# A two-layer graph network on one core: the per-group sums, one-hots and window finishing are placed ahead of VectorE's wait for the gathered rows, and half of the attribute products behind the V products

## The chip, the core and the metric

The kernel runs on one core of a Trainium2 chip. A core has TensorE (PE in the profile; PEld is its weight loading), VectorE (DVE), ScalarE (ACT), GpSimd (POOL) and the sync engine SP, which here only issues DMAs. Each engine runs its own program in order and waits on semaphores. The metric is the device time of one execution in microseconds. Before the change it is 3113.4 us, the median of three runs (3105.56 to 3114.23).

## What is computed

A graph of 6250 nodes with 128 features and 200,000 edges sorted by destination. Layer 0 is a graph attention layer with 4 heads; layer 1 sums edge attributes and neighbours and runs a two-layer perceptron. Cut to what matters:

```python
h = relu(layernorm(x))                              # layer 0
xp = (h @ W).reshape(n, 4, 32)                      # the rows called V
e = leaky_relu(a_s[src] + a_d[dst], 0.2)            # self loops are added to the edges
e = exp(e - segment_max(e, dst)[dst])
out = segment_sum(e * xp[src], dst) / segment_sum(e, dst)
x = x + relu(out + bias)
h = relu(layernorm(x))                              # layer 1
edge_agg = segment_sum(edge_attr @ We + be, dst)
x_comb = concatenate([h, edge_agg])
z = x_comb + segment_sum(x_comb[src], dst)
x = x + relu(z @ W1 + b1) @ W2 + b2
```

## The kernel before the change

The program first makes the table of rows xp with their logits, then runs over the edges in 87 groups, and at the end multiplies a stored adjacency matrix with the layer-1 rows (49 windows, the last stage). The change lies in the loop over groups; everything else stays.

A group is 2304 edges, laid out as 128 partitions by J = 18 columns. Since the edges are sorted, the destinations of a group fall in a window of 128 nodes, and neighbouring groups' windows overlap, so the running sums of a window are loaded from DRAM, changed and stored again by each group. Buffers of V, AT (attributes), SEL (the one-hot matrix) and node alternate between two (b is n mod 2); `state`, the 128 x 261 tile of a window's running sums, exists once. Its columns are 128 weighted feature sums, 4 sums of weights and a count (133, `TAB`), and 128 attribute sums (to `ST` = 261).

For group n the work goes like this:

- POOL gathers the rows of V with 18 indirect DMAs. Its last ones (j = 14, 15, 16) wait until the V products of group n - 1 have passed each of their three quarters (`vm_b`).
- DVE waits for the gather, copies the logits (`logit`) and runs a segmented maximum over them: a scan, a carry across partitions by way of PE (`tailT`, `tails`, `cback`), and a second scan. The peaks are split into three bf16 parts, and PE reduces them into the window's nodes (`mg`, 18 matmuls with the one-hot `selH`).
- DVE makes the new shifts (`newold`, `nu`, `node`) and splits them. PE looks them up for each edge (`look`, 18 matmuls with `selT`). DVE and ACT turn them into weights (`lks`, `lin`, `lre`, `wps`), and DVE multiplies V by them in three quarters (`vw_b`).
- PE sums by one-hot matmuls: the attribute products (`attribute_sums`, L1133: SEL times AT, 18 columns in fp32, two passes each in the trace) and the V products (L1194: SEL times V). Between them stand chunks of the adjacency matrix (`adjacency`, L1123 and L1125), each evacuated by ACT.
- When group n + 1 is under way, DVE finishes group n: `rescale_state` multiplies the loaded state by the fold factors, `add_sums` adds the products (`merged`), and a chain of small dependent steps (`finish_weights` to `finish_shift`, with three Newton rounds for a reciprocal square root) makes the next layer's rows.

In the kernel before, DVE does all of this behind the logit copy of group n + 1, woven between the steps of the maximum: `select` and `rescale_state` stand behind the first scan, `add_sums` behind the `tails` scan, and the finishing steps one by one between the later ones.

SP's program sets when transfers start. In an item it issues in this order: store of the state of n - 1 (waits for `merged`), store of the new peaks, indices for n + 2, peaks and rows for n + 1 (waits for `look`), **the attributes for n + 2** (L453, 1152 KB, waits for `am_b` of group n, the end of the attribute products), **the state of group n** (L502, 130.5 KB), x of the window (L505), and then the stores of the finished rows and of the adjacency block. The order is that of the code:

```python
if ahead is not None:
    load_attributes(n + 2, b, ahead)    # after(sp, s("am_b"), n, 2)
...
load_sums(n, base)                      # state <- sums0
```

`rescale_state(n)` in turn begins with two waits:

```python
dve.wait_ge(s("s_load"), n * 16 + 16)   # the state of group n has landed
after(dve, s("fold_b"), n)
```

## Time and profile before

| | |
|---|---|
| median of 3 runs | 3113.4 us (3105.56 to 3114.23) |
| the profiled execution | 3102.13 us, span 3100.2 us |
| PE busy, DVE busy | 66%, 58% of the span |
| ACT busy, POOL busy | 35%, 54% |
| mean granted TensorE clock | 0.764 of full speed |
| moved by DMA | 560.29 MB, mean 181 GB/s |
| group loop | 87 groups, about 2.5 ms of the span |
| last stage | from about 2660 us to the end |

Busy time is time in which an engine has an instruction running. Where an engine is neither full nor empty, what counts is which wait ends last in each group. A timeline row shows start, duration, engine, line and tiles, and in brackets the idle time before it with what ended it. Rows of matmuls are merged with their count (x30 is 15 columns of two passes).

### The profile page before, as it was taken

What the parts mean: (1) busy time and instruction counts of PE and PEld (TensorE: products, weight loads), DVE (VectorE), ACT (ScalarE), POOL (GpSimd) and SP (SyncE); (2) the same over time, 40 slices, a digit from 0 to 9 for tenths busy, and PEclk for the clock granted to TensorE, in tenths of its full rate; (3) what the DMA queues carried; (4) which work ended last, traced back from release to release, by engine and by line L of the source; (5) the groups of instructions that cost most, each with busy time, mean ns of one, the idle gap of its engine ahead of it and who ended that gap; (6) DMA issues with size and microseconds to landing.
All of it is one profiled execution on the core that took longest, in us unless ns stands there. A gap on an engine that the chain in (4) does not pass through costs nothing.

```text
span 3100.2 us, 64216 instructions
## 1 busy us (share of the span) xinstructions
PE 2043.0 (66%) x16208; PEld 1674.9 (54%) x16208; DVE 1807.2 (58%) x6198; ACT 1085.6 (35%) x2295; POOL 1673.2 (54%) x1626
## 2 busy tenths in 40 slices
PE   4365665665665655665656656656656656699998
PEld 3354554554554544554545545545545544588887
DVE  7566676665666666666666766766766766411111
ACT  3134344344434443443443443443444443300000
POOL 4566666666666666666666666666666666000000
PEclk8677777776777767777767777777777777799999
DMA  9855655655655555655556556556556555666654
GB/s 192 134 163 177 194 168 174 195 159 180 193 155 187 177 169 189 189 160 185 162 176 194 157 184 194 168 173 194 156 185 194 156 185 176 225 213 214 225 212 146
DMA packets 276907, 560.29 MB, mean 181 GB/s; under 512 B 113395, under 2 KB 211139, under 8 KB 248081
## 3 DMA queue, kind: packets, MB, share of 16 engines
q1 hardware_dynamic: 226763, 444.37, 42.5%
q0 software_dynamic: 50112, 115.56, 16.5%
q8 instruction: 12, 0.20, 0.0%
q14 instruction: 20, 0.16, 0.0%
HBM read 382.53 MB, written 177.22 MB: 181 GB/s over the span
## 4 chain that ended last, share of the span: by engine, by line
PE 41%; issue 20%; DVE 15%; DMA 9%; another core or an unknown queue 5%; SPq 3%; ACT 2%; POOL 2%; ACTq 1%; DVEq 1%; POOLq 0%
PE pv L1133 10%; PE pv L1248 9%; DMA big<-table,idx 8%; PE pv L1194 7%; PE pt L1248 4%; PE pt L1123 3%; PE pm L1161 2%; POOL big L816 2%; ACT xsb L852 2%; PE pa L1123 1%; DVE peaks L1513 1%; DVE tabb L1477 1%; PE pa L1177 1%; ACTq L905 1%
## 5 line engine op out<-in xcount | busy, mean ns | idle before, releaser
L816 POOL DMA_INDIRECT big<-table,idx x1566 | 1639.8, 1047 | 929.9 <-issue 414.2
L852 ACT ACTIVATE xsb<-pt 128x343 f32 x1042 | 477.8, 459 | 1213.3 <-PE pt L1125 567.1
L1133 PE MATMUL pv<-big 128*128 128x128 f32 x3132 | 523.6, 336 | 5.7 <-ACT big L852 3.5
L1133 PEld LDWEIGHTS pv<-big 128*128 128x128 f32 x3132 | 490.3, 246 | 36.1 <-issue 11.7
L1123 PE MATMUL pt<-tabb 128*128 128x343 bf16 x1042 | 400.0, 384 | 65.8 <-ACT xsb L852 36.5
L1194 PE MATMUL pv<-big 128*128 128x133 f32 x3132 | 391.3, 280 | 7.0 <-DVE big L1742 4.2
L1638 DVE COPY logit<-big 128x72 f32<-128x72 f32 x87 | 21.9, 252 | 608.6 <-DMA big<-table,idx 540.1
L1194 PEld LDWEIGHTS pv<-big 128*128 128x128 f32 x3132 | 367.8, 190 | 16.2 <-DVE big L1742 8.6
L1477 DVE TENSOR_TENSOR tabb<-iotah,keyp 128x2064 bf16<-128x2064 bf16 x261 | 319.7, 1225 | 0.0
L1142 PE MATMUL pm<-ident,pre 128*4 128x128 f32 x87 | 32.5, 374 | 433.9 <-DVE pre L1643 226.5
L1248 PE MATMUL pv<-big,xsb 128*128 128x384 bf16 (+1 forms) x1617 | 279.3, 330 | 18.5 <-DVE big L1779 18.5
L852 ACT ACTIVATE xsb<-pa 128x343 f32 x521 | 238.9, 458 | 95.0 <-ACT xsb L852 50.3
L1248 PEld LDWEIGHTS pv<-big,xsb 128*128 128x128 bf16 (+1 forms) x1617 | 230.4, 147 | 52.4 <-issue 21.4
L1142 PEld LDWEIGHTS pm<-ident,pre 128*4 128x4 f32 x87 | 7.2, 82 | 451.5 <-DVE pre L1643 236.4
L1742 DVE TENSOR_TENSOR big<-big,pm 128x768 f32<-128x768 f32 x261 | 233.4, 949 | 26.2 <-ACT pm L852 18.7
L1125 PE MATMUL pt<-tabb 128*128 128x49 bf16 x1041 | 224.9, 216 | 0.0
L1123 PE MATMUL pa<-tabb 128*128 128x343 bf16 x521 | 200.8, 385 | 28.3 <-issue 18.3
L1161 PE MATMUL pm<-peaks,selb 128*128 128x13 bf16 x1566 | 56.2, 174 | 228.8 <-DVE peaks L1513 143.7
L1123 PEld LDWEIGHTS pt<-tabb 128*128 128x128 bf16 x1042 | 114.9, 110 | 159.5 <-ACT xsb L852 63.1
L1161 PEld LDWEIGHTS pm<-peaks,selb 128*128 128x128 bf16 x1566 | 48.5, 105 | 261.2 <-DVE peaks L1513 157.2
L852 ACT ACTIVATE big<-selb 128x2304 f32<-128x2304 bf16 x87 | 184.1, 2116 | 1.0 <-DVE selb L1477 1.0
L852 ACT ACTIVATE fhT<-pt,b1s 128x128 f32<-128x128 f32 (+1 forms) x49 | 18.0, 367 | 388.6 <-PE pt L1225 388.6
(289 smaller groups left out, 2975.8 us busy)
## 6 DMA issues: line engine op xcount, KB each, us to landing
adj<-xsb SPq DMA_DIRECT2D x87, 1568.0 KB
big<-in_edge_attr_dram SPq DMA_DIRECT2D x87, 1152.0 KB
xsb<-adj SPq DMA_DIRECT2D x33, 1568.0 KB, 6.2
selb<-rel SPq DMA_DIRECT2D x87, 576.0 KB
tabb<-adj SPq DMA_DIRECT2D x16, 1568.0 KB, 6.2
big<-table,idx POOLq DMA_INDIRECT x1566
state<-sums SPq DMA_DIRECT2D x87, 130.5 KB
sums<-state SPq DMA_DIRECT2D x87, 130.5 KB
```

Source lines behind the costliest of these rows:

```text
L816: pool.indirect_dma_start(out=V[b][:, j, 0:rows], out_offset=None, in_=table, in_offset=bass.IndirectOffsetOnAxis(ap=index[b][:, j:j + 1], ...
L852: return nc.scalar.activation(out_, in_, func, **kw).then_inc(s(name), 1)
L905: _, at = nc.values_load_multi_w_load_instructions(offs[0:1, bass.DynSlice(n * OW + lo, hi - lo)], engines=[mybir.EngineType.Activation], ...
L1123: ins = nc.tensor.matmul(pab[c % 3], ohl[:, c, :], ohk[:, c, 0:KW], start=True, stop=alone)
L1125: ins = nc.tensor.matmul(pab[c % 3][:, 0:NB], ohl[:, (c - 1) % J, :], ohc[:, (c - 1) % J, 0:NB], start=False, stop=True)
L1133: ins = nc.tensor.matmul(sumA[b], SEL[b][:, j, :], AT[b][:, j, :], start=(j == 0), stop=(j == J - 1))
L1142: nc.tensor.transpose(tailT, pre1[:, :, J - 1], ident[:, :]).then_inc(s("tailT_b"), 1)
L1161: ins = nc.tensor.matmul(mg, selH[:, j, :], peaks[:, j, :], start=(j == 0), stop=(j == J - 1))
L1194: ins = nc.tensor.matmul(sumV[b], SEL[b][:, j, :], V[b][:, j, 0:TAB], start=(j == 0), stop=(j == J - 1))
L1248: ins = nc.tensor.matmul(pay[k][0:rows, 0:NK * C], adjT[k][:, 0:rows, h], yb[:, h, :], start=(h == 0), stop=(h == NB - 1))
L1477: return v.tensor_tensor(to.rearrange("p j (w e) -> p j w e", e=2), v_in, at, ALU.is_equal)
L1742: v.tensor_tensor(v4, v4, wps[:, js, :].rearrange("p j (h a) -> p j h a", a=1) .to_broadcast([128, QUART, H, F]), ALU.mult).then_inc(s("vw ...
```

## The change

Three things change in the code of a group.

1. The attribute sums get a PSUM bank of their own (`pc`), a single one in place of two halves of the alternating V banks. So the first attribute product of group n waits until group n - 1 is merged (before: n - 2), and the merge is two additions, one of 133 columns from `pv` and one of 128 columns from `pc`; the second waits for `am_b`.
2. Of the 18 attribute columns, 9 to 17 go behind the V products; `am_b` is signalled there.
3. On DVE `select`, the copy of the last-of-segment marks, `rescale_state`, `add_sums`, `finish_projection` and all finishing steps go ahead of the wait for the gathered rows.

```diff
@@ -286,7 +286,7 @@
         sumV = [pv[b][:, 0:TAB] for b in range(2)]
-        sumA = [pv[b][:, TAB:ST] for b in range(2)]
+        sumA = pc[:, 0:C]
@@ -1130,7 +1130,7 @@
                     for j in range(lo, hi):
-                        ins = nc.tensor.matmul(sumA[b], SEL[b][:, j, :], AT[b][:, j, :],
+                        ins = nc.tensor.matmul(sumA, SEL[b][:, j, :], AT[b][:, j, :],
                                                start=(j == 0), stop=(j == J - 1))
@@ -1165,7 +1165,7 @@
-                after(pe, s("merged"), n, 2)
+                after(pe, s("merged"), n, 1)
                 attribute_sums(0, 3)
@@ -1179,7 +1179,7 @@
-                attribute_sums(3, J).then_inc(s("am_b"), 1)
+                attribute_sums(3, 9)
                 if finish_before:
                     transpose_window(n - 1)
@@ -1194,6 +1194,7 @@
                     ins.then_inc(s("vm_b"), 1)
+                attribute_sums(9, J).then_inc(s("am_b"), 1)
                 if not is_extra:
                     adjacency(n, 9, 15)
@@ -1532,8 +1533,11 @@
             def add_sums(n, b):
                 dve.wait_ge(s("vm_b"), n * QN + QN)
-                dve.wait_ge(s("ms_b"), n * 2 + 2)
-                v.tensor_tensor(state[:, :], state[:, :], pv[b][:, 0:ST], ALU.add).then_inc(s("merged"), 1)
+                dve.wait_ge(s("ms_b"), n * 3 + 2)
+                v.tensor_tensor(state[:, 0:TAB], state[:, 0:TAB], pv[b][:, 0:TAB], ALU.add).then_inc(s("ms_b"), 1)
+                after(dve, s("am_b"), n)
+                dve.wait_ge(s("ms_b"), n * 3 + 3)
+                v.tensor_tensor(state[:, TAB:ST], state[:, TAB:ST], sumA, ALU.add).then_inc(s("merged"), 1)
@@ -1634,6 +1638,22 @@
+                select(n, b, extra_group)
+                last = isl[:, bass.DynSlice(g, 1), :].rearrange("p a (j c) -> p (a j) c", c=1)
+                v.tensor_copy(peaks[:, :, NK * H:NK * H + 1], last).then_inc(s("pkl_b"), 1)
+                if m is not None:
+                    rescale_state(m, 1 - b)
+                    add_sums(m, 1 - b)
+                if not (is_extra or (isinstance(n, int) and n < 2)):
+                    finish_projection(n - 2)
+                for step in (finish_weights, finish_mean, finish_bias, finish_residual, finish_stats,
+                             finish_variance, finish_eps, finish_halve, finish_guess, finish_b2):
+                    between(step)
+                for r in range(3):
+                    between(newton_square, r)
+                    between(newton_factor, r)
+                    between(newton_step, r)
+                between(finish_shift)
                 dve.wait_ge(s(f"gat{b}"), it * 16 * J + 16 * J)
                 v.tensor_copy(logit[:, :, :], V[b][:, :, C:C + H].rearrange("p j h -> p h j"))\
                     .then_inc(s("log_b"), 1)
@@ -1643,81 +1663,52 @@
-                select(n, b, extra_group)
-                if m is not None:
-                    rescale_state(m, 1 - b)
                 after(dve, s("thru_c"), n)
                 after(dve, s("tailT_b"), n)
                 v.tensor_tensor_scan(tails[:, 1:129], thruT[:, :], tailT, -BIG, ALU.add, ALU.max)\
                     .then_inc(s("tails_b"), 1)
-                if m is not None:
-                    add_sums(m, 1 - b)
-                if not (is_extra or (isinstance(n, int) and n < 2)):
-                    finish_projection(n - 2)
-                between(finish_weights)
-                between(finish_mean)
...
-                between(newton_step, 2)
-                between(finish_shift)
```

On DVE, the order around the wait for the gathered rows of the second group (the semaphores waited for stand in brackets; `gat1` is the gather, `s_load` the landing of the state). Before:

```order
L1635 TENSOR_SCALAR cont<-isl 128x4x17
L1638 COPY logit<-big 128x72 [waits gat1]
L1643 SCALAR_TENSOR_TENSOR pre<-cont,logit 128x72 [waits log_b,cont_b]
L1477 TENSOR_TENSOR selb<-iotah,drp 128x2304 [waits selc_b,mg_b]
L1528 TENSOR_TENSOR state<-state,fold 128x128 [waits fold_b,s_load]
L1530 TENSOR_TENSOR state<-state,fold 128x4
L1651 SCALAR_TENSOR_TENSOR tails<-thruT,pm 4x128 [waits tailT_b,thru_c]
L1536 TENSOR_TENSOR state<-state,pv 128x261 [waits ms_b,vm_b]
L1545 RECIPROCAL frd<-state 128x4 [waits merged]
```

The same place now, up to the first finishing steps; the logit copy comes only behind all of them:

```order
L1639 TENSOR_SCALAR cont<-isl 128x4x17
L1478 TENSOR_TENSOR selb<-iotah,drp 128x2304 [waits selc_b,mg_b]
L1643 CAST peaks<-isl 128x18
L1529 TENSOR_TENSOR state<-state,fold 128x128 [waits fold_b,s_load]
L1531 TENSOR_TENSOR state<-state,fold 128x4
L1537 TENSOR_TENSOR state<-state,pv 128x133 [waits ms_b,vm_b]
L1540 TENSOR_TENSOR state<-state,pc 128x128 [waits ms_b,am_b]
L1549 RECIPROCAL frd<-state 128x4 [waits merged]
L1551 COPY fdeg<-state 128x1
L1555 TENSOR_TENSOR fo<-state,frd 128x128 [waits fin]
```

The waits for `s_load` and `am_b` now stand in front of the wait for the gather, on the same engine.

On PE, the place behind the last quarter of V products in a group of the first pair (`pc` is the new bank, L1133 the attribute products, L1123 and L1125 the next adjacency chunk):

```order
 L1114 MATMUL pa<-wew,fhT 128x128
 L1194 MATMUL pv<-big 128x133 x6
+L1133 MATMUL pc<-big 128x128 x9
 L1123 MATMUL pt<-tabb 128x343
 L1125 MATMUL pt<-tabb 128x49
```

Nine columns of attribute products have come between the V products and the adjacency chunks.

SP's order is the same in both programs. The part of it on which the state load depends:

```order
L491 DMA selb<-rel 128x2304 [waits look]
L453 DMA big<-in_edge_attr_dram 128x2304 [waits am_b]
L502 ISA [waits ftr_f,s_store]
L502 DMA state<-sums 128x261
L505 ISA [waits x1_f]
L505 DMA fxw<-in_x_dram 128x128
```

Nothing moved here, but `am_b` is now signalled later.

## Rows read from the trace of the kernel before

**Rows 1.** Of the page: busy time and share of each engine
```profile
PE 2043.0 (66%) x16208; PEld 1674.9 (54%) x16208; DVE 1807.2 (58%) x6198; ACT 1085.6 (35%) x2295; POOL 1673.2 (54%) x1626
```

**Rows 2.** Of the page, costliest groups: columns are busy us, mean ns, idle before
```profile
L1638 DVE COPY logit<-big 128x72 f32<-128x72 f32 x87 | 21.9, 252 | 608.6 <-DMA big<-table,idx 540.1
```

**Rows 3.** Instructions on the tile state (ns min/median/max, first to last start)
```profile
L1528 DVE TENSOR_TENSOR state<-state,fold x87: 277/284/293, 152.1 to 2650.4; 128x128 f32<-128x128 f32 x87
...
DMA to landing us min/median/max: 1.7/5.4/12.2
```

**Rows 4.** Timeline of DVE, one group (start us, duration us, [idle before])
```profile
1528.42 0.22 DVE L1638 COPY logit<-big 128x72 f32<-128x72 f32 x1 [8.10 <-DMA big<-table,idx]
...
1528.98 1.34 DVE L1477 TENSOR_TENSOR selb<-iotah,drp 128x2304 bf16<-128x2304 bf16 x1
...
1530.51 0.40 DVE L1651 TENSOR_TENSOR_SCAN tails<-thruT,pm 4x128 f32<-4x128 f32 x1
...
1541.43 0.61 DVE L1725 TENSOR_REDUCE lks<-pa 128x144 f32<-128x432 f32 x1 [0.88 <-remote]
...
1543.44 2.68 DVE L1742 TENSOR_TENSOR big<-big,pm 128x768 f32<-128x768 f32 x3 [0.30 <-ACT pm L852]
...
1557.36 0.22 DVE L1638 COPY logit<-big 128x72 f32<-128x72 f32 x1 [7.39 <-DMA big<-table,idx]
```

**Rows 5.** Timeline of PE, the same group
```profile
1529.12 0.38 PE L1142 MATMUL pm<-ident,pre 128*4 128x128 f32 x1 [5.24 <-DVE pre L1643]
...
1530.97 0.59 PE L1144 MATMUL pm<-ident,tails 4*128 4x4 f32 x2 [1.48 <-issue]
...
1536.18 1.62 PE L1133 MATMUL pv<-big 128*128 128x128 f32 x6 [0.24 <-ACT big L852]
...
1538.29 0.66 PE L1177 MATMUL pa<-node,selb 128*128 128x24 bf16 x18 [0.49 <-DVE node L1511]
...
1539.76 4.87 PE L1133 MATMUL pv<-big 128*128 128x128 f32 x30
...
1545.20 2.97 PE L1194 MATMUL pv<-big 128*128 128x133 f32 x24
...
1548.45 1.53 PE L1194 MATMUL pv<-big 128*128 128x133 f32 x12
```

**Rows 6.** Timeline of ACT, the same group
```profile
1533.82 2.12 ACT L852 ACTIVATE big<-selb 128x2304 f32<-128x2304 bf16 x1
```

**Rows 7.** Timeline of SP's queue, the same group
```profile
1546.53 0.33 SPq L453 DMA_DIRECT2D big<-in_edge_attr_dram  x1
1547.21 0.33 SPq L502 DMA_DIRECT2D state<-sums  x1
```

**Rows 8.** Of the page, DMA issues: KB each, last number median us to landing
```profile
xsb<-adj SPq DMA_DIRECT2D x33, 1568.0 KB, 6.2
```

**Rows 9.** Timeline of SP's queue in the last stage
```profile
2740.93 0.34 SPq L593 DMA_DIRECT2D xsb<-adj  x1
2741.91 0.33 SPq L597 DMA_DIRECT2D state<-sums  x1
```

**Rows 10.** Windows of the last stage: engines, clock, DMA share, GB/s
```profile
2744.00:2745.00 1.00, 1.00 (x8) 0.87 (x7) 0.00 (x0) 0.00 (x0) 0.00 (x0) 1.00 0.94 401
```

**Rows 11.** Timeline of SP's queue, group 86 (no attribute load ahead of it)
```profile
2648.26 0.35 SPq L502 DMA_DIRECT2D state<-sums  x1
```

**Rows 12.** Timeline of DVE behind the last group
```profile
2650.40 0.29 DVE L1528 TENSOR_TENSOR state<-state,fold 128x128 f32<-128x128 f32 x1
...
2653.21 0.43 DVE L1536 TENSOR_TENSOR state<-state,pv 128x261 f32<-128x261 f32 x1 [2.44 <-PE pv L1194]
...
2658.28 0.16 DVE L1609 SCALAR_TENSOR_TENSOR fnm<-fmv,fy 128x1 f32<-128x1 f32 x1
```

**Rows 13.** Windows of the group: third number from the end is PEclk
```profile
1525.00:1526.00 1.00, 0.00 (x0) 0.00 (x0) 0.00 (x0) 0.27 (x1) 0.70 (x2) 0.69 0.97 376
...
1542.00:1543.00 1.00, 1.00 (x9) 1.00 (x8) 0.86 (x5) 0.66 (x3) 0.82 (x1) 0.78 0.46 92
```

More of the change, by code:

```diff
@@ L1661, in item @@
                                        in1=logit[:, :, 0], op0=ALU.add, op1=ALU.max).then_inc(s("carry_b"), 1)
-                between(finish_bias)
                 after(dve, s("carry_b"), n)
@@ L1666, in item @@
                     .then_inc(s("pre2_b"), 1)
-                between(finish_residual)
-                last = isl[:, bass.DynSlice(g, 1), :].rearrange("p a (j c) -> p (a j) c", c=1)
-                v.tensor_copy(peaks[:, :, NK * H:NK * H + 1], last).then_inc(s("pkl_b"), 1)
                 after(dve, s("pre2_b"), n)
@@ L1672, in item @@
                                 last.to_broadcast([128, J, H]), ALU.mult).then_inc(s("pk_b"), 1)
-                between(finish_stats)
                 split_peaks(n, 0)
-                between(finish_variance)
                 split_peaks(n, 1)
-                between(finish_eps)
                 split_peaks(n, 2)
-                between(finish_halve)
                 split_peaks(n, 3)
-                between(finish_guess)
                 if not is_extra:
@@ L1684, in item @@
                     v.tensor_scalar(selT, selT, ranko[:, 0:1], None, ALU.is_equal).then_inc(s("selt_b"), 1)
-                between(finish_b2)
-                between(newton_square, 0)
                 after(dve, s("mg_b"), n)
@@ L1692, in item @@
                                 AX.X, ALU.add).then_inc(s("mgs_b"), 1)
-                between(newton_factor, 0)
                 dve.wait_ge(s("st_load"), n * 32 + 32)
@@ L1698, in item @@
                     .then_inc(s("mnew_b"), 1)
-                between(newton_step, 0)
                 after(dve, s("mnew_b"), n)
@@ L1704, in item @@
                                 ALU.add).then_inc(s("nu_b"), 1)
-                between(newton_square, 1)
                 after(dve, s("nu_b"), n)
@@ L1708, in item @@
                                        op0=ALU.mult, op1=ALU.max).then_inc(s("sh_b"), 1)
-                between(newton_factor, 1)
                 split_shift(n, b, 0)
-                between(newton_step, 1)
                 split_shift(n, b, 1)
-                between(newton_square, 2)
                 split_shift(n, b, 2)
-                between(newton_factor, 2)
                 split_shift(n, b, 3)
```

## Prediction

> **What bounds the kernel now.** I read the busy shares first: no engine is full, PE has 66% and DVE 58% [rows 1]. So a group's time is a chain of waits, and I looked for the waits that end last. DVE sits idle before the logit copy for 608.6 us in 87 groups, 7.0 us each, nearly all of it released by the gather [rows 2]. The state tile's first rescale runs once a group, from 152.1 to 2650.4 us: 86 intervals of 29.05 us [rows 3]. Then I took one group of the timelines apart, from logit copy (T) to logit copy, 28.94 us:
>
> - T = 1528.42 to the lookup matmuls (L1177) at 1538.29: 9.87 us [rows 4, 5].
> - Lookups to the first V product (L1194) at 1545.20: 6.91 us [rows 5].
> - First V product to the next logit copy at 1557.36: 12.16 us, in which DVE waits 7.39 us for the gather [rows 4, 5].
>
> The state load is nowhere in this chain. It is issued at 1547.21 [rows 7], and the state is first needed behind the 1.34 us one-hot that follows the next logit copy [rows 4].
>
> **The change, part by part.**
>
> *Finishing ahead of the gather.* Behind T less work stands between the steps of the maximum. PE's transpose of the scan (L1142) ends at 1529.12 + 0.38 = 1529.50, but the tails scan starts only at 1530.51, behind the 1.34 us one-hot and the rescale [rows 4, 5]. Without them it starts at about 1529.52: 0.99 us won. From there ACT and PE bind. The carry matmul (L1144) starts at 1530.97; ACT's copy of the one-hot ends at 1533.82 + 2.12 = 1535.94; the first attribute products start at 1536.18 and take 1.62 us, so the lookups can't start before 1537.80, that is 0.49 us ahead of today's 1538.29 [rows 5, 6]. The rest of the moved work, some 5 us of DVE time, gains nothing more, since that copy ends last. Together 9.87 - 0.99 - 0.49 = 8.4 us from T to the lookups.
>
> *Half of the attribute products behind the V products.* DVE is ready with the first quarter of V 1541.43 - 1538.29 = 3.14 us (lookup read) + 2.01 us (to 1543.44) + a third of 2.68 us = 6.0 us behind the lookups [rows 4, 5]; with its signal 6.1 us. Today PE comes at 6.91 us, because 30 attribute passes of 4.87 us stand before [rows 5]. With 12 passes there DVE binds: 6.1 us, 0.8 won. The V products take 1548.45 - 1545.20 + 1.53 = 4.78 us, unchanged. Behind them now come 18 passes of 2.97/24 = 0.124 us (the spacing of the 24 V passes, which run at the full clock [rows 5]): 2.2 us. So `am_b` comes 7.0 us behind the first V product; today it comes at 1539.76 + 4.87 = 1544.63, which is 0.6 us ahead of it. It is 7.6 us later against the V products, 6.8 us against the lookups.
>
> *What hangs on am_b.* SP waits for it before the attribute load and issues the state load only behind that. DVE now waits for the state, and for `am_b` itself, ahead of the logit copy. Queued behind that wait on DVE are the merge, all finishing steps, the logit copy and the whole softmax chain, and PE, ACT and SP wait for these. From am_b on:
>
> - am_b to the issue of the attribute load: 1546.53 - 1544.63 = 1.9 us here [rows 5, 7]. SP had other work before in some groups, so I take 1.2 us, from both sides 0.5 and 2.0.
> - Attribute load to landing. A 1568 KB load lands a median of 6.2 us behind its issue [rows 8]; at the 401 GB/s of a full microsecond [rows 10] the 416 KB less take 1.0 us off: 5.2 us for 1152 KB.
> - The state load follows 0.68 us behind on the same queue [rows 7]. Alone it takes at most 2.1 us: issued at 2648.26 with no attribute load ahead, used at 2650.40 [rows 11, 12]. Loads of state behind a large load land in a median of 5.4 us, 1.7 to 12.2 [rows 3]; one is issued 0.98 us behind such a load [rows 9], so it lands 6.4 us behind it, right after the large load's own 6.2. I take 5.2 + 0.3 = 5.5 us behind the attribute load's issue. The ends for the range are 0.68 + 2.1 = 2.8 us and, by the long landings, about 8.5 us.
> - 0.2 us until DVE starts, an estimate.
> - DVE from the rescale to the logit copy. Behind the last group the same steps stand alone: from the addition at 2653.21 to the last step at 2658.28 is 5.07 us [rows 12]. Before them come the rescale (0.4 us to the first addition) and a second addition (0.3 us). Together 5.8 us.
>
> First V product to logit copy: 7.0 + 1.2 + 5.5 + 0.2 + 5.8 = 19.7 us, against 12.16 today. The gather is ready at 12.16 as before and is hidden.
>
> The Trainium skill (DMA: Bandwidth & Descriptors, Queues, rings and completion order) says that each DMA engine takes the descriptors of one ring in order; the trace agrees, with 6.4 us for the small load against 6.2 for the large one. Its table of measured transfers (same page, Bandwidth) gives 6.15 us of transfer for 1 MB, and its anatomy of a DMA a fixed 2.0 us. By these the state would land more than 8 us behind the attribute load's issue, and the group would be near 37 us. The trace has 6.2 us in all for a larger load, and decides.
>
> *The sum.* A group takes 8.4 + 6.1 + 19.7 = 34.2 us, 5.3 more than 28.94. Two of the 86 intervals have no attribute load ahead of their state load; I count 84 x 5.3 = 445 us and 4 us for those two. On the profiled execution's 3102 us that gives 3551 us. The median of the runs, 3113.4, is 11 us above that execution, less than a term's error. I predict 3550 us.
>
> *Cost nothing.* The second addition is in the sum. The one bank instead of two makes the first attribute product wait for the merge of the group before, which DVE now does ahead of the logit copy: long done. The adjacency chunks behind the last attribute products come 2.2 us later and end some 11 us behind the first V product, under the wait of 19.7 us; if that cover were gone they would cost those 2.2 us.
>
> **The rivals.**
>
> *B, the state lands early.* If the small load isn't held up by the large one, it lands 2.8 us behind the attribute load's issue and not 5.5: 31.5 us a group, 3102 + 84 x 2.6 = 3320 us. For it: the 2.1 us of the last group. Against: the 6.4 us of the last stage.
>
> *C, a slower landing or a slower clock.* The attribute load now meets the last gathers and the adjacency store, or PE stays at the low clock. PE's granted clock falls to 0.69 and then half while PE is idle behind a group and rises only at 1542 us, in the attribute products [rows 13]. With less work between lookups and V products it may rise later, and 24 V passes at half speed cost 3 us more. 3 us a group on top of mine: 3102 + 84 x 8.3 = 3800 us.
>
> *D, faster: the gather still ends last.* Then only the gains count: 8.4 + 6.1 + 12.16 = 26.7 us a group, 3102 - 84 x 2.3 = 2910 us. It decides if the state is on chip 5.8 us before the gather's data, 6.4 us behind the first V product. For it: DVE's 7.0 us of idle time hold the 5 us of moved work. Against: `am_b` alone comes at 7.0 us, and the load behind it.
>
> *E, gain and loss cancel.* The state lands at once (about 2 us behind a quick issue) and gains after T are larger than I think, through less queueing on DVE: 29 us a group, 3100 us.
>
> **How the numbers follow.** My case 0.65, B 0.12, C 0.14: slower in all three, 0.91. D 0.05 is faster, E 0.04 is split, about half of it within the 0.3% (9 us) that a measurement of this kernel can tell from no change. So faster 0.06, same 0.02, slower 0.92. The range: 3390 to 3740 us. Its low end has the state landing 3.5 us behind the attribute load's issue; its high end 7.8 us. It leaves out the ends of B and C.
>
> **What would show it.** In the profile after: DVE's idle time moves from the logit copy, where it vanishes, to the rescale and is released by the DMA of the state, about 9 us a group. SP's attribute load is issued about 8 us behind the first V product and not 1.3. Lookups start 8.4 us behind the logit copy, V products 6.1 us behind the lookups. The low clock lasts for more of the group. I am wrong if the gather still releases the logit copy, if the state lands within 3 us of its issue, or if the interval of the rescale rows stays under 31 us.

## The result and the profile after

| | before | after |
|---|---|---|
| median | 3112.24 us (3105.56 to 3114.23) | 3361.18 us (3353.99 to 3365.96, 4 runs) |
| ratio | | 1.0801, 95% interval 1.0774 to 1.0829 |
| state rescale to state rescale, mean of 86 | 29.05 us [rows 3] | 32.03 us |
| DVE's idle time ahead of the logit copy | 608.6 us [rows 2] | none among the page's groups |

The kernel became slower, as forecast and by the forecast wait, but by 249 us and not by 437: the time lies 29 us below the range of 3390 to 3740 us.

Busy times hardly moved on PE (2043.0 before [rows 1]), and DVE has 210 us more; its finishing steps now stand one behind the other with nothing between them, but I didn't test that reason:

```profile
PE 2049.6 (61%) x16208; PEld 1675.0 (50%) x16208; DVE 2017.8 (60%) x6285; ACT 1055.3 (31%) x2295; POOL 1724.2 (51%) x1626
```

The page's costliest groups have no row for the logit copy any more. The idle time is now ahead of the rescale of the state:

```profile
L1529 DVE TENSOR_TENSOR state<-state,fold 128x128 f32<-128x128 f32 x87 | 25.7, 296 | 527.1 <-issue 271.7
```

"issue" says only that the profile shows no releaser. The view of the tile `state` splits the 527 us. Its landing times are, as in [rows 3], those of the last stage alone: the profile gives a landing for the 49 loads of 64 KB there (L597) and for none of the 87 loads of 130.5 KB in the loop. So they say nothing about the change; the loop's own loads are judged below by when they are used:

```profile
L1529 DVE TENSOR_TENSOR state<-state,fold x87: 284/293/366, 157.1 to 2911.9; 128x128 f32<-128x128 f32 x87
...
  issue: 271.7, 45
  DMA state<-sums: 255.4, 40
...
DMA to landing us min/median/max: 1.8/5.3/12.2
```

One group after, on PE (start, duration, instruction, idle before). The last 18 attribute passes (L1133) stand behind the V products (L1194) and end at 1536.32, 6.80 us behind the first V product:

```profile
1523.53 0.68 PE L1177 MATMUL pa<-node,selb 128*128 128x24 bf16 x18
...
1529.52 2.99 PE L1194 MATMUL pv<-big 128*128 128x133 f32 x24 [0.77 <-issue]
1532.79 1.53 PE L1194 MATMUL pv<-big 128*128 128x133 f32 x12
1534.15 2.17 PE L1133 MATMUL pc<-big 128*128 128x128 f32 x18
```

SP's queue in the same group. The attribute load comes 0.17 us behind the last pass, the state load 0.65 us behind that:

```profile
1536.49 0.33 SPq L453 DMA_DIRECT2D big<-in_edge_attr_dram  x1
1537.14 0.25 SPq L502 DMA_DIRECT2D state<-sums  x1
```

DVE from the previous logit copy on. It waits 5.95 us for the state, does both additions and all finishing steps, and then copies the logits with no wait:

```profile
1515.54 0.21 DVE L1658 COPY logit<-big 128x72 f32<-128x72 f32 x1
...
1526.49 0.61 DVE L1716 TENSOR_REDUCE lks<-pa 128x144 f32<-128x432 f32 x1 [1.26 <-remote]
...
1542.38 0.29 DVE L1529 TENSOR_TENSOR state<-state,fold 128x128 f32<-128x128 f32 x1 [5.95 <-DMA state<-sums]
...
1548.30 0.22 DVE L1658 COPY logit<-big 128x72 f32<-128x72 f32 x1
```

One group misleads about sizes, as this case will show, so I took means over the 54 to 68 groups between 600 and 2400 us in each trace (`am_b` is the end of the last attribute pass). In us:

| | before | forecast | after |
|---|---|---|---|
| logit copy to lookups | 10.55 | 8.4 | 8.14 |
| lookups to first V product | 6.62 | 6.1 | 5.21 |
| first V product to `am_b` | -0.68 | 7.0 | 6.80 |
| `am_b` to attribute load | 1.27 | 1.2 | 0.16 |
| attribute load to rescale | | 5.7 | 5.95 |
| rescale to logit copy | | 5.8 | 5.99 |
| first V product to logit copy | 12.11 | 19.7 | 18.89 |
| group | 29.29 | 34.2 | 32.25 |

Two of the signs that the prediction named came out smaller. DVE's idle time ahead of the rescale is 6.1 us a group (527.1/87) and not 9: in the group above DVE has work of its own until 6.9 us behind the first V product. And TensorE's clock hardly changed: its mean between 600 and 2400 us is 0.73 of full speed before and 0.72 after.

### The profile page after: what moved, and what is told of

It reads as the page before. It is cut to its first block, busy times and chain, and to the rows that moved or that the text cites. A ratio compares the mean times of both kernels' runs of the same rounds, so it can differ in the third digit from the quotient of the medians.

```text
span 3362.6 us, 64390 instructions
## 1 busy us (share of the span) xinstructions
PE 2049.6 (61%) x16208; PEld 1675.0 (50%) x16208; DVE 2017.8 (60%) x6285; ACT 1055.3 (31%) x2295; POOL 1724.2 (51%) x1626
## 4 chain that ended last, share of the span: by engine, by line
PE 31%; DVE 30%; issue 20%; DMA 7%; SPq 4%; ACT 3%; another core or an unknown queue 2%; DVEq 1%; ACTq 1%
PE pv L1249 8%; DVE tabb L1478 7%; PE pc L1133 6%; DMA state<-sums 6%; PE pv L1194 5%; PE pt L1249 4%; PE pm L1161 2%; DVE selb L1478 2%; PE pt L1123 2%; DVE big L1733 2%; PE pm L1144 2%; ACT big L852 2%; DVE fy L1600 1%; DVE tails L1668 1%
## 5 line engine op out<-in xcount | busy, mean ns | idle before, releaser
L816 POOL DMA_INDIRECT big<-table,idx x1566 | 1690.7, 1080 | 1140.5 <-PE pm L1144 448.8
L1133 PE MATMUL pc<-big 128*128 128x128 f32 x3132 | 530.6, 332 | 56.9 <-ACT big L852 49.7
L1133 PEld LDWEIGHTS pc<-big 128*128 128x128 f32 x3132 | 487.0, 242 | 100.1 <-issue 54.1
L1123 PE MATMUL pt<-tabb 128*128 128x343 bf16 x1042 | 402.0, 386 | 59.7 <-ACT xsb L852 36.6
L1194 PE MATMUL pv<-big 128*128 128x133 f32 x3132 | 393.6, 280 | 36.1 <-DVE big L1733 24.2
L1194 PEld LDWEIGHTS pv<-big 128*128 128x128 f32 x3132 | 369.4, 191 | 51.2 <-DVE big L1733 32.0
L1529 DVE TENSOR_TENSOR state<-state,fold 128x128 f32<-128x128 f32 x87 | 25.7, 296 | 527.1 <-issue 271.7
L1125 PE MATMUL pt<-tabb 128*128 128x49 bf16 x1041 | 225.9, 217 | 0.0
L1123 PE MATMUL pa<-tabb 128*128 128x343 bf16 x521 | 201.9, 387 | 25.2 <-ACT xsb L852 23.9
L1123 PEld LDWEIGHTS pt<-tabb 128*128 128x128 bf16 x1042 | 116.9, 112 | 151.8 <-ACT xsb L852 63.4
L1783 DVE TENSOR_TENSOR fy<-pa,fxw 128x128 f32<-128x128 f32 (+1 forms) x49 | 14.3, 292 | 227.3 <-PE pa L1233 227.3
L1478 DVE TENSOR_TENSOR tabb<-iotah,lop 128x768 bf16<-128x768 bf16 x261 | 144.5, 554 | 0.0
## 6 DMA issues: line engine op xcount, KB each, us to landing
state<-sums SPq DMA_DIRECT2D x87, 130.5 KB
sums<-state SPq DMA_DIRECT2D x87, 130.5 KB
```

The source lines that it names most:

```text
L816: pool.indirect_dma_start(out=V[b][:, j, 0:rows], out_offset=None, in_=table, in_offset=bass.IndirectOffsetOnAxis(ap=index[b][:, j:j + 1], ...
L1123: ins = nc.tensor.matmul(pab[c % 3], ohl[:, c, :], ohk[:, c, 0:KW], start=True, stop=alone)
L1125: ins = nc.tensor.matmul(pab[c % 3][:, 0:NB], ohl[:, (c - 1) % J, :], ohc[:, (c - 1) % J, 0:NB], start=False, stop=True)
L1133: ins = nc.tensor.matmul(sumA, SEL[b][:, j, :], AT[b][:, j, :], start=(j == 0), stop=(j == J - 1))
L1194: ins = nc.tensor.matmul(sumV[b], SEL[b][:, j, :], V[b][:, j, 0:TAB], start=(j == 0), stop=(j == J - 1))
L1478: return v.tensor_tensor(to.rearrange("p j (w e) -> p j w e", e=2), v_in, at, ALU.is_equal)
```

## The experiments

The chips differ. The first pair above ran at 3112 us before; in the experiments the kernel before took 2857 us (e1 to e4), 2834 (e5, e6, c_after, c_before), 3111 (e7 to e10) and 3107 (e11 to e13, c2_before). So each ratio is to the runs of before on the same chip. I call the chips with 2857 and 2834 us the quick ones, the others the slow ones. c2_before ran on the chip of e11 to e13; where e7 to e10 are set against it below, it is another slow chip.

| run | median us | ratio (95%) | logit copy to lookups | to V | to logit copy |
|---|---|---|---|---|---|
| c_before | 2841.09 | | 9.06 | 5.87 | 11.26 |
| c_after | 3286.77 | 1.161 (1.156 to 1.166) | 8.13 | 4.35 | 18.91 |
| e1_state_first | 3232.07 | 1.130 (1.127 to 1.133) | 8.12 | 4.17 | 18.43 |
| e2_state_first_am | 3457.24 | 1.209 (1.206 to 1.212) | 8.12 | 4.61 | 20.46 |
| e3_attr_ahead | 2859.75 | 1.001 (0.999 to 1.003) | 8.16 | 6.52 | 11.54 |
| e4_dve_old | 2992.61 | 1.046 (1.043 to 1.049) | 9.28 | 5.12 | 13.43 |
| e5_small_first | 2938.40 | 1.038 (1.033 to 1.042) | 8.16 | 4.55 | 14.60 |
| e6_small_first_attr_ahead | 3054.06 | 1.078 (1.073 to 1.082) | 8.15 | 6.43 | 14.07 |
| c2_before | 3101.89 | | 10.51 | 6.64 | 12.11 |
| e7_merge_ahead | 3129.03 | 1.006 (1.004 to 1.008) | 10.08 | 7.20 | 12.20 |
| e8_before_adj_early | 3137.51 | 1.009 (1.006 to 1.011) | 12.38 | 6.83 | 10.45 |
| e9_merge_adj_early | 3147.20 | 1.012 (1.010 to 1.015) | 11.99 | 7.12 | 10.61 |
| e10_small_adj_early | 3090.06 | 0.993 (0.991 to 0.996) | 10.00 | 6.09 | 12.89 |
| e13_small_adj_again | 3089.94 | 0.994 (0.992 to 0.996) | 10.00 | 6.10 | 12.90 |
| e11_before_gate4 | 3225.62 | 1.038 (1.034 to 1.043) | 9.05 | 5.91 | 15.57 |
| e12_small_adj_gate6 | 3404.52 | 1.096 (1.091 to 1.102) | 9.91 | 8.21 | 14.34 |

### c_after and c_before: both kernels on one quick chip

> The changed kernel itself, on the chip of this set, as the yardstick for the others. All theories: 1.07 to 1.12 times the kernel before, and groups in which VectorE waits ahead of the rescale for the DMA of the state. It also says whether the shorter stretches of the last set (4.2 us from lookups to V products, 5.2 in the changed kernel's first profile) belong to the kernel or to the chip.

> The kernel before, unchanged, for a profile on this chip: ratio 1.00. The groups should take 26 us if the chip is like that of the last set (2857 us in all) and 29 us if it is like that of the first profile (3102 us).

The loss is 1.161 here, above the 1.07 to 1.12 that I expected, and 1.080 on the first chip. The changed kernel has the same chain from V products to logit copy on both, 18.91 and 18.89 us, and here the profile puts all 539.6 us of idle time ahead of the rescale down to the DMA of the state. The kernel before varies most: 26.20 us a group here, 29.29 there. The shorter stretch from lookups to V products, 4.35 against 5.21 us, belongs to the chip.

### e1: the state load ahead of the attribute load

```diff
+load_sums(n, base)
 if ahead is not None:
     load_attributes(n + 2, b, ahead)
-load_sums(n, base)
```

> The changed kernel, with SP issuing the state load of group n ahead of the attribute load for n + 2, so that it waits neither for the end of the attribute products nor in the queue behind 1152 KB. My theory (the group's new end is the state load, issued behind am_b and landing behind the attribute load): DVE's wait moves off the rescale, the group is 8.1 us (logit copy to lookups) + 5.2 (to the V products) + 12.5 (to the next logit copy, the later of the gather at 12.1 and the merge at 6.8 + 5.6 us of finishing) = 25.8 us in place of 32.0, and the time about 2830 us. Rival 1 (six microseconds of dependent finishing steps ahead of the logit copy are the loss by themselves, whenever the state lands): above 3250 us. Rival 2 (half of the attribute products behind the V products is the loss, since the merge waits for them): above 3200 us.

The wait for the state is gone, yet the ratio is still 1.130, and 3232 us is the number of rival 2. The trace shows another cause. A second wait took the place of the first, in `finish_projection`, of the page's groups:

```profile
L1620 DVE SCALAR_TENSOR_TENSOR fy<-bew,fdeg,pa 128x128 f32<-128x128 f32 x87 | 30.2, 347 | 490.5 <-DMA sums<-fy 487.5
```

That step may overwrite `fy` only when the store of the finished rows is complete, and SP issues this store behind the attribute load. One group on SP and DVE:

```profile
1527.73 0.33 SPq L453 DMA_DIRECT2D big<-in_edge_attr_dram  x1
1528.30 0.35 SPq L515 DMA_DIRECT2D resid<-fxb  x1
1529.54 0.35 SPq L520 DMA_DIRECT2D sums<-fy  x1
```

```profile
1527.40 0.28 DVE L1529 TENSOR_TENSOR state<-state,fold 128x128 f32<-128x128 f32 x1
1528.18 0.29 DVE L1540 TENSOR_TENSOR state<-state,pc 128x128 f32<-128x128 f32 x1
1533.98 0.35 DVE L1620 SCALAR_TENSOR_TENSOR fy<-bew,fdeg,pa 128x128 f32<-128x128 f32 x1 [5.50 <-DMA sums<-fy]
```

In the changed kernel this second gate is hidden by the first: DVE is idle for 7.9 us in all ahead of the same step.

### e2: the state load first, but still behind am_b

```diff
 after(sp, s("ftr_f"), n, 1)
+after(sp, s("am_b"), n)
 sp.dma_start(state[:, :], sums0[...])
```

> As the kernel with the state load first, but the state load still waits for am_b. So it takes away only the queueing behind the attribute load. My theory: from am_b the rescale comes after 0.25 us + about 2.1 us of a lone load + 0.3 us in place of 6.2 us, 3.5 us less a group: about 3060 us. If small loads don't queue behind large ones (the landing takes 5 us for another reason): as the changed kernel, 3361 us. If the finishing chain or the split is the loss: also near 3361 us.

1.209, slower than the change itself, where I had expected it 9% faster: both gates stand one behind the other. The group also prices the queue. The state load, issued ahead of the attribute load, is used 2.17 us behind its issue (1511.57 - 1509.40); in the changed kernel, 0.65 us behind it, 5.24 us (1542.38 - 1537.14). The means over the groups are 2.20 and 5.28 us:

```profile
1509.40 0.33 SPq L503 DMA_DIRECT2D state<-sums  x1
...
1510.44 0.52 SPq L453 DMA_DIRECT2D big<-in_edge_attr_dram  x1
```

```profile
1511.57 0.29 DVE L1530 TENSOR_TENSOR state<-state,fold 128x128 f32<-128x128 f32 x1 [2.94 <-DMA state<-sums]
...
1517.19 0.35 DVE L1621 SCALAR_TENSOR_TENSOR fy<-bew,fdeg,pa 128x128 f32<-128x128 f32 x1 [4.53 <-DMA sums<-fy]
```

So 3.1 us of the landing is the large load ahead. The Trainium skill (DMA: Bandwidth & Descriptors, Queues, rings and completion order) has descriptors of one ring taken in order; these two rows agree.

### e3 and e4: each half of the change alone

e3 has all attribute products ahead of the V products, the rest as in the change. e4 has the split, with VectorE's order of before.

```diff
-attribute_sums(3, 9)
+attribute_sums(3, J).then_inc(s("am_b"), 1)
...
-attribute_sums(9, J).then_inc(s("am_b"), 1)
```

> The changed kernel with all 18 attribute columns ahead of the V products again (own bank and VectorE's new order kept), so am_b comes about 0.6 us before the first V product. My theory: the state load is issued 6 us earlier, the rescale comes about 7 us behind the first V product and the logit copy at 13.0; 8.1 + 6.6 + 13.0 = 27.7 us a group, about 2990 us. Rival (the finishing chain ahead of the logit copy is the loss): above 3300 us.

> The changed kernel with VectorE's order of before (one-hot, sums and finishing behind the logit copy), but the split attribute products, the own bank and the two additions kept. My theory: the state lands about 13.5 us behind the first V product, just ahead of its rescale at 13.9, so the late load is nearly hidden; 10.5 + 5.2 + 12.1 to 12.6 = 27.8 to 28.3 us a group, about 3010 us. Rival (the split is the loss): above 3200 us.

The times that I expected were for a chip of 3112 us; as ratios they are 0.96 for e3 and 0.97 for e4, and for the rivals above 1.06 and above 1.03. e3 loses nothing (1.001): without the late `am_b` the finishing work fits into the wait for the gather. It gains nothing either. Against c_before (another quick chip) its 0.9 us behind the logit copy is given back: 0.65 between lookups and V products, where PE has 30 attribute passes to do, and 0.28 behind the V products, where DVE waits 92.0 us in all for the state and only 11.6 us for the gather, so that the finishing steps end last by a little. In e4 the ratio is the rival's: the split alone loses 4.6%, with no wait for the state on the page. The gather itself comes later, 13.43 us behind the V products against 11.54 in e3 on the same chip.

```profile
L1642 DVE COPY logit<-big 128x72 f32<-128x72 f32 x87 | 20.8, 239 | 677.1 <-DMA big<-table,idx 677.1
```

GpSimd has issued its last gather nearly as early (8.4 us behind the first V product, 8.1 in e3), but the logits are copied 5.0 us after that in e4 and 3.4 in e3. The attribute load now runs beside the last gathers, and the store of the adjacency block has come later too. In the change this cost is hidden behind the state.

### e5 and e6: all small transfers ahead of the attribute load

```diff
+load_sums(n, base)
+store_residual(n - 1, base_before)
+store_projected(n - 2, base_of(n - 2))
 load_attributes(n + 2, b, ahead)
-load_sums(n, base)
-...
```

e5 is the changed kernel with this order, e6 is e3 with it.

> The changed kernel with every small transfer (state load, x of the window, the two stores of finished rows) issued by SP ahead of the attribute load. My theory, widened after the last set: VectorE's new order waits for two things that SP queues with the attribute load, the landing of the state and the completion of the last y store (sums<-fy), 5.5 us of idle in the kernel with the state first. With both ahead of it the rescale and the finishing find no wait: 8.1 us to the lookups + 4.2 to 5.2 to the V products + 12.3 to the next logit copy (am_b at 6.8, then 5.5 us) = 24.6 to 25.6 us a group, 0.94 to 0.98 of the kernel before; if the late attribute load slows the gather as it seems to in the kernel with the old VectorE order (13.4 us behind the first V product), 25.8 us and 0.99. Rival (the finishing chain ahead of the logit copy is the loss by itself): 1.05 or more.

> The same SP order, and all attribute products ahead of the V products. My theory: nothing of VectorE's new order waits for a transfer; the logit copy comes at the later of the gather and vm_b + 5.4 = 10.2 us behind the first V product; 8.1 + 6.5 + 10.3 to 11 = 25 to 25.6 us a group, 0.95 to 0.99 of the kernel before. Rival (the finishing chain is the loss): 1.00 to 1.05, as with the attributes ahead alone or worse.

e5 takes both gates away and is left with the gather: from 1.161 to 1.038, V to logit copy 18.91 to 14.60. That is most of the loss. The ratio lies between my 0.94 to 0.99 and the rival's 1.05; without its 2.2 us a group of waiting for the gather, DVE's own steps would still end 12.3 us behind the first V product. Its page:

```profile
L1658 DVE COPY logit<-big 128x72 f32<-128x72 f32 x87 | 21.2, 243 | 193.9 <-DMA big<-table,idx 193.9
```

e6 I had wrong. Its `am_b` is early, but SP now sits at the small transfers, and the attribute load comes 3.5 us behind `am_b` (0.16 in e3); the gather is ready 14.07 us behind the V products, and the ratio is 1.078. This is the cleanest view of what a late attribute load does to a gather: GpSimd has issued the last gather at the same time as in e3 (8.2 and 8.1 us behind the first V product), and SP issues the adjacency store at the same time (4.1 and 4.2 us). Only the attribute load comes some 3.1 us later, and the logits are copied 5.9 us behind the last gather and not 3.4. An early `am_b` is worth nothing if SP isn't there to use it.

### e7 to e10: fewer steps ahead, the adjacency store early

e7 is e3 with the finishing steps woven behind the logit copy again. e8 is the kernel before with one move, e9 is e7 and e10 is e5 with the same move:

```diff
 load_rows(n + 1)
+store_adjacency(n - 1, 1 - b)
 load_attributes(n + 2, b, ahead)
...
-store_adjacency(n - 1, 1 - b)
```

> The kernel of e3 (all attribute products ahead of the V products, the sums in a bank of their own), but only the one-hot, the marks, the rescale and the two additions stand ahead of VectorE's wait for the gather; the finishing steps are woven behind it as in the kernel before. Theory G (what is gained behind the logit copy is given back between lookups and V products while 30 attribute passes stand there, because TensorE binds there): T to lookups 8.3 to 8.6, lookups to V products 6.3 to 6.6, first V product to the next logit copy 11.3, 26.2 us a group: ratio 0.99 to 1.00, as e3. Rival M (the placement of the small steps counts, e3 lost by DVE's queue): 25.5 us a group, ratio 0.97.

> The kernel before, with one edit: SP issues the store of the adjacency block of group n - 1 right behind the load of the one-hot rows (released by the lookups of group n) and not at the end of its item, so it moves some 5 us ahead of the first V product and the attribute load stands behind it. Theory T (the last gathers are held up by large transfers that run beside them): the gather lands 9.7 to 10.5 us behind the first V product and not 11.3, a group takes about 25.2 us, ratio 0.95 to 0.97. Rival P (the gather's end is set by POOL's own issuing and by vm_b alone): V to logit copy stays at 11.3, ratio 0.995 to 1.005.

> e7 and e8 together. Theory T with G: T to lookups 8.4, lookups to V 6.5, V to logit copy 10, ratio 0.94 to 0.97. Rival P: as e7, 0.99 to 1.00. A third outcome: the attribute load, now behind the adjacency store in SP's queue, lands late and with it the state: DVE waits for the state at the rescale and the ratio is over 1.02.

> e5 (the changed kernel, with state, x, residual and y ahead of the attribute load in SP's order) with the adjacency store moved as in e8. In e5 the gather landed 14.6 us behind the first V product. Theory T (the adjacency store and the late attribute load meet the last gathers): with the store gone ahead only 1152 KB of 2720 KB still run beside them, the gather lands at 11.5 to 13 us behind V, 8.15 + 4.5 + 12.3 = 25 us a group, ratio 0.94 to 0.99. Rival P: V to logit copy stays at 14.6, ratio 1.03 to 1.04.

e7 (1.006) did not gain: against c2_before 0.4 us is won behind the logit copy and 0.6 lost between lookups and V products, as theory G has it, but late signals (below) blur both. In e8 the gather ends last (511.8 us of idle time ahead of the logit copy) and came as theory T said, 10.45 us behind the V products and not 12.11, though GpSimd has issued the last gather at nearly the same time (8.1 and 8.2 us behind the first V product): a large transfer beside the last gathers delays them by 1.5 to 1.7 us. In e10 the gather is hidden (14.4 us of idle time in all); DVE's own steps end at 12.89 us, so the gather came no later than that, against 14.60 in e5 (on a quick chip). In e9 DVE waits 279.1 us for the state, the third outcome, though the ratio is 1.012 and not over 1.02. But in e8 and e9 more than the gain was lost behind the logit copy: 12.4 and 12.0 us to the lookups, 10.5 in the kernel before. So both missed their ratios of 0.94 to 0.97. One group of e8 shows how. GpSimd issues gathers without a pause, and then PE and DVE see signals late, DVE even its own:

```profile
1516.64 0.95 POOL L816 DMA_INDIRECT big<-table,idx  x1 [0.30 <-issue]
1517.90 0.95 POOL L816 DMA_INDIRECT big<-table,idx  x1 [0.30 <-issue]
1519.15 0.94 POOL L816 DMA_INDIRECT big<-table,idx  x1 [0.30 <-issue]
1523.21 0.94 POOL L816 DMA_INDIRECT big<-table,idx  x1 [3.12 <-PE pm L1161]
```

```profile
1512.39 0.22 DVE L1638 COPY logit<-big 128x72 f32<-128x72 f32 x1 [6.57 <-DMA big<-table,idx]
...
1518.61 0.15 DVE L1585 TENSOR_SCALAR fy<-fve 128x1 int32<-128x1 int32 x1 [0.72 <-DVE fve L1581]
1519.33 0.25 DVE L1513 TENSOR_TENSOR peaks<-pkr,peaks 128x72 bf16<-128x72 f32 x1 [0.56 <-DVE peaks L1511]
1520.72 0.15 DVE L1590 TENSOR_SCALAR fy<-fy 128x1 int32<-128x1 int32 x1 [1.14 <-remote]
```

```profile
1521.45 0.65 PE L1161 MATMUL pm<-peaks,selb 128*128 128x13 bf16 x18 [4.84 <-issue]
```

PE's merge of the peaks starts 1.87 us behind the end of the DVE step it waits for (1519.33 + 0.25); in the group of before it started 0.06 us behind (1534.29 against 1533.98 + 0.25). e10 is the only version that beats the kernel before, by 0.7% (interval 0.4 to 0.9%), just short of the 1 to 6% that I expected.

### e11, e12, e13: a shorter burst of gathers

```diff
-if j == 8:
+if j == 4:
     pool.wait_ge(s("mg_b"), n)
```

e11 is the kernel before with this edit, e12 is e10 with 6 in place of 8, e13 is e10 again.

> The kernel before, with one edit: GpSimd's eighth gather no longer waits for the merged peaks, the fourth does, so GpSimd is quiet from about 2 us behind the logit copy until the peaks are merged. On chips where before takes 3111 us VectorE, TensorE and ScalarE see signals 1 to 3 us late some 7 us behind the logit copy, at the end of a burst of nine gathers; where it takes 2840 us they don't. Theory L (the lateness comes with the burst of gathers): on a chip of the first kind T to lookups falls from 10.5 to about 9.1 us, with no idle time released by remote ahead of the reading of the peaks; on one of the second kind it stays at 9.1. Rival S (it comes with small stores such as the state's, 3 us behind the logit copy): stays at 10.5. In both the gathers come 2 to 3 us later, so V to logit copy grows from 11.3 or 12.1 to 13 to 15 and the ratio is 1.0 to 1.08; the reading counts here, not the ratio.

> e10 (the changed kernel with the small transfers and the adjacency store ahead of the attribute load) with the sixth gather waiting for the merged peaks and not the eighth: a burst of six or seven gathers and not of nine. Theory L: on a chip of the slow kind T to lookups falls from 10.0 to 8.2 to 9 us, V to logit copy grows by at most 0.5 us, ratio to before 0.95 to 0.98; on the fast kind nothing is late and the ratio equals that of e13. Rival S: as e13 on either.

> The kernel of e10 once more, beside the two others. On a chip of the kind where before takes 3111 us: 0.993 as measured. On one where it takes 2840 us theory L has no late signals, so 8.15 us from logit copy to lookups, 4.4 to the V products, 12.9 to the next logit copy: 25.5 us against 26.2, ratio 0.97 to 0.98. Rival: the ratio is 0.993 there too.

> The kernel before, unchanged, for its trace on this chip: 26.2 us a group and T to lookups 9.1 if this chip is of the kind of 2840 us, 29.3 and 10.5 if it is of the kind of 3111 us.

e11 hit theory L on its reading: 9.05 us from logit copy to lookups, against 10.51 in c2_before on the same chip, with nothing late there. All lines of DVE, reading of the merged peaks (idle before it and its releasers), c2_before and then e11:

```profile
L1689 DVE TENSOR_SCALAR pen<-pm 128x1 f32<-128x1 f32 x87 | 13.7, 157 | 63.3 <-remote 34.4 <-PE pm L1161 26.4
```

```profile
L1689 DVE TENSOR_SCALAR pen<-pm 128x1 f32<-128x1 f32 x87 | 13.1, 151 | 0.1
```

The state store, rival S, is issued at the same 3.0 us behind the logit copy in both. The gathers came later, as expected, and the ratio is 1.038. But the lateness moved with them: the attribute load is issued 2.3 us behind `am_b` (1.1 in c2_before), and the V products take 9.1 us from first to last and not 4.8. There it isn't only signals that are late. PE waits for nothing between the products of one quarter, and still three in a row start 0.7 us apart:

```profile
1308.13 0.27 PE L1194 MATMUL pv<-big 128*128 128x133 f32 x1 [0.70 <-issue]
1308.86 0.27 PE L1194 MATMUL pv<-big 128*128 128x133 f32 x1 [0.45 <-issue]
1309.57 0.41 PE L1194 MATMUL pv<-big 128*128 128x133 f32 x2 [0.44 <-issue]
```

e12 missed: 1.096 where I had 0.95 to 0.98. Fewer gathers ahead of the merged peaks means more of them behind, and the lateness moved there: 8.21 us from lookups to V products against 6.10 in e13, and 6.39 from first to last V product against 4.79. So in e11 and e12 the lateness went with the gathers and wasn't removed by shifting them. e13 repeats e10 on another slow chip (0.994).

## Why the forecast was right and where it was wrong

**Direction and mechanism: right.** `am_b` comes 6.8 us behind the first V product, the attribute load is issued there, and the state load behind it. DVE waits for the state and not for the gather. That the split makes it so is shown by e3 (without it, no loss), that the transfers' places in the queue matter by e2 and e5.

**What failed: two terms of the sum, both read off one group.** Together they are 1.93 of the 1.95 us a group by which the forecast was too high.

**The first failed step is "am_b to the issue of the attribute load".** I took 1.2 us, with ends of 0.5 and 2.0; it is 0.16. That is 1.04 us a group, 89 us, and it lay outside my ends. The prediction explained the 1.9 us of the group it read by other work of SP. The trace of before doesn't bear that out. In that group SP issued its last earlier load 2.7 us ahead of the end of the attribute products (1544.63):

```profile
1541.57 0.33 SPq L491 DMA_DIRECT2D selb<-rel  x1
```

In all 62 groups between 600 and 2400 us that load had been issued at least 1.1 us ahead. And on the quick chip the same program needs 0.16 us: the attribute products end at 1517.41 + 3.59 = 1521.00, the load is issued at 1521.17:

```profile
1517.41 3.59 PE L1133 MATMUL pv<-big 128*128 128x128 f32 x30
1521.17 0.33 SPq L453 DMA_DIRECT2D big<-in_edge_attr_dram  x1
```

So what I priced was the lateness that the slow chips show, in a place of the group where it occurs. At the new place of `am_b` it doesn't: 0.16 us in every group on the slow chip too, though GpSimd is still issuing gathers there, the last one 8.2 us behind the first V product. Why not there stays open.

**The second is "lookups to first V product": 6.1 us forecast, 5.21 measured**, 0.89 us a group, 77 us. In it I kept the 3.14 us from the lookups to their use on DVE; the mean is 2.94 before and 1.88 after. A late signal is part of it, but not of the difference. It is as large after as before (idle time ahead of the use, before and then after):

```profile
L1725 DVE TENSOR_REDUCE lks<-pa 128x144 f32<-128x432 f32 x87 | 52.8, 607 | 69.5 <-remote 68.5 <-PE pa L1177 0.9
L1716 DVE TENSOR_REDUCE lks<-pa 128x144 f32<-128x432 f32 x87 | 52.8, 607 | 68.5 <-remote 65.9 <-PE pa L1177 1.0 <-issue 0.4
```

What changed is the work in front of it. Between the new shifts and the use of the lookups DVE makes three one-hots for the adjacency matrix, 2 us of work. Before they ended 2.19 us behind the start of the lookups, after 1.10 us (2.02 and 0.74 on the quick chip of c_before and c_after). With the finishing steps gone from behind the logit copy DVE has the shifts ready earlier, while ACT's copy and the first attribute products still hold up the lookups on PE. The prediction saw that hold-up and concluded that the rest of the moved work "gains nothing more, since that copy ends last". It gains about 1.1 us, one stage later: DVE's one-hots now overlap with PE's delay. In turn the way from there to the first V product was 0.4 us longer than I took it.

**The smaller terms.** Logit copy to lookups 8.14 for 8.4, V product to `am_b` 6.80 for 7.0, landing 5.95 for 5.7, rescale to logit copy 5.99 for 5.8; they cancel. The means differ by 1.95 us, 168 us in 86 groups. The remaining 21 us of the 189 are mostly that the whole loop averages 32.03 us and not the 32.25 of the middle part. The landing was in part luck: the median of 5.4 us that I took from [rows 3] belongs to loads of 64 KB in the last stage, and the state loads of the loop have 130.5 KB.

**The landing was right, and with it the rivals' fate.** B (the small load isn't held up) falls by e2: 2.20 us against 5.28 in the mean. Nor did the more than 8 us come that the prediction had as its other estimate: the state is in use 5.95 us behind the issue of the attribute load. C did not come: the state landed no later, and the V products kept their pace (4.79 us from first to last, 4.78 before) at the full clock. E (29 us a group) did not come either. D's condition, that the gather ends last, is met in e4 to e8 and not in the change; and even then the kernel isn't faster, since the gather itself comes later (e4 to e6) or the gains behind the logit copy are given back (e7, e8).

**What I did not see.** The store of the finished rows is a second gate behind the same load (e1); the state hid it. And a late attribute load costs the gather some 2 us even where nobody waits for the state (e4, e6). Both are hidden in the changed kernel, but a repair that moves the state load alone runs into the first, and one that moves all small transfers into the second.

**The range.** Its ends are the doubt about the landing, 3.5 to 7.8 us. Neither of the two terms that failed moved them, though 0.5 us was my own low end for the first.

What stays open: what makes signals and instructions late, and why on some chips and not on others. That it is the gathers is argued from where it occurs (e8, e11, e12), not shown: c_before issues the same bursts at the same pace of 1.25 us with nothing late, and the changed kernel has a signal on time in the middle of them. Whether e10 gains more than 0.7% on a quick chip wasn't tried.

## What to carry to other kernels

A signal that releases a large load also releases everything queued behind that load. Before you move it, list what stands behind it on the issuing queue, loads and stores both, and who waits for each; here nine columns of matmuls were moved, and the state and the finished rows went with them. Take each term of a chain as a mean over many groups, and before you call a delay an engine's backlog, look at what that engine last did. When a step can't start earlier, ask what the engine behind it does with the time: its other work may move under the wait.

## What the runs showed of the hardware

- A load of 130.5 KB is used 2.17 us behind its issue with nothing large ahead of it (e2) and 5.24 us when a 1152 KB load stands 0.65 us ahead of it on SP's queue (after).
- The kernel before takes 2834 to 2857 us on two chips and 3107 to 3112 us on the others, with the same program: 26.2 against 29.3 us a group, 1.5 of it between logit copy and lookups.
- On the slower ones signals come late in stretches in which gathers are issued: DVE waits 0.6 us for its own signal (e8), and `am_b` takes up to 3.8 us to SP (e11; 0.16 us on the quick chip). Matmuls that wait for nothing start late too (e11). With a pause in the gathers none is late in the stretch behind the logit copy (e11). In the changed kernel `am_b` reaches SP on time, in 0.16 us, while gathers are issued.
- A 1568 KB store moved away from the last gathers lets them land 1.7 us earlier (e8 against before); a 1152 KB load issued 3.1 us later lets them land at least 2.5 us later (e6 against e3).
